# A cross-attention and mixture-of-experts layer: output tiles handled inside the last attention turns, and another way to list the experts' tokens

## The reference, cut to what matters

```python
# x (16, 112, 256); context (16, 375, 256); 16 heads of 16; 8 experts, 256 -> 512 -> 256
x = x + attention(layernorm(x), ctx, ctx, mask, Wq, bq, Wk, bk, Wv, bv, Wo, bo)
flat = layernorm(x).reshape(1792, 256)
probs = softmax(flat @ router_w)                      # (1792, 8)
topk_w, topk_idx = top_k(probs, 2);  topk_w /= clip(sum(topk_w), 1e-9)
y_e = silu(flat @ w1[e]) @ w2[e]                      # expert e
x = x + sum over the two chosen experts of weight * y_e
```

## Time and profile before

| | |
|---|---|
| median of 3 runs | 522.26 us (521.93 to 522.46) |
| the profiled execution | 520.47 us |
| its span, first to last instruction | 518.3 us |
| PE busy | 424.2 us, 82% |
| DVE, ACT, POOL busy | 348.9, 262.6, 189.3 us |
| mean granted TensorE clock | 0.896 of full |
| chain that ended last | PE 74%, DVE 9%, DMA 4%, ACT 4%, POOL 2% |

### The profile page before, as it was taken

One profiled execution on the slowest core, in us unless ns is written; L12 is line 12 of the kernel. 1 busy time (PEld: TensorE's weight loads), 2 busy tenths in 40 slices (PEclk: granted clock), 3 DMA queues, 4 the chain that ended last, 5 costly groups with the idle time before them and its releaser, 6 DMA issues.

```text
span 518.3 us, 10586 instructions
## 1 busy us (share of the span) xinstructions
PE 424.2 (82%) x4151; PEld 391.1 (75%) x4151; DVE 348.9 (67%) x743; ACT 262.6 (51%) x338; POOL 189.3 (37%) x162
## 2 busy tenths in 40 slices
PE   2666689999999999999996758445799999999800
PEld 2454489999999999999885657345799999999800
DVE  2776557788788788877871296474667667777427
ACT  3230245666666566666555204101877777777500
POOL 8270462222222222222100430007277777776410
PEclk9796779999999999999999687655999999999965
DMA  7949658676666677775604398002022222221158
GB/s 179 220 145 282 181 149 161 136 143 148 134 146 136 147 152 151 151 151 124 122 4 145 103 393 307 10 1 81 32 82 83 92 82 90 84 91 63 52 166 289
DMA packets 60609, 70.08 MB, mean 135 GB/s; under 512 B 19313, under 2 KB 55681, under 8 KB 60561
## 3 DMA queue, kind: packets, MB, share of 16 engines
q1 hardware_dynamic: 48224, 48.18, 39.8%
q0 software_dynamic: 4032, 11.02, 6.3%
q10 hardware_dynamic: 8304, 10.23, 5.6%
HBM read 35.64 MB, written 15.04 MB: 98 GB/s over the span
## 4 chain that ended last, share of the span: by engine, by line
PE 74%; DVE 9%; issue 5%; DMA 4%; ACT 4%; POOL 2%; SPq 1%; POOLq 0%; DVEq 0%; ACTq 0%
PE ps L1268 39%; PE ps L1329 11%; PE ps L1344 9%; PE ps L1358 8%; PE ps L1558 2%; ACT probs L678 2%; DMA y_back<-y_rows 2%; PE ps L1371 1%; SPq L477 1%; DVE x_rows_sb L927 1%; PE ps L1548 1%; DVE neg_max L880 1%; PE ps L1508 1%; DVE stats L916 1%; PE ps L1381 1%
## 5 line engine op out<-in xcount | busy, mean ns | idle before, releaser
L880 DVE TENSOR_REDUCE neg_max<-ps 112x1 f32<-112x376 f32 x256 | 133.7, 545 | 39.1 <-PE ps L1329 34.0
L678 ACT ACTIVATE probs<-ps 125x1344 f32<-125x1344 f32 x64 | 82.7, 1292 | 42.4 <-PE ps L1344 36.5
L1329 PE MATMUL ps<-k_stack,q_stack 98*112 98x376 f32 x256 | 89.2, 383 | 10.1 <-issue 6.0
L508 POOL TENSOR_TENSOR k_lo<-k_f,k_hi 128x752 fp32r<-128x752 f32 x16 | 28.8, 1802 | 139.2 <-ACT k_hi L652 136.7
L617 POOL DMA_INDIRECT y_rows<-y_out,slot_of_row x42 | 53.2, 1266 | 37.2 <-ACT y_out L814 30.8
L609 POOL DMA_INDIRECT rows<-xn_rows,token_of_row x42 | 42.9, 1021 | 61.2 <-DVE token_of_row L1142 47.5
L1329 PEld LDWEIGHTS ps<-k_stack,q_stack 98*112 98x112 f32 x256 | 45.7, 181 | 24.1 <-DVE neg_max L880 13.4
L1344 PE MATMUL ps<-q_stack,k_stack 100*125 100x224 f32 x384 | 53.6, 276 | 3.3 <-ACT probs L678 3.0
L1344 PEld LDWEIGHTS ps<-q_stack,k_stack 100*125 100x125 f32 x384 | 51.2, 191 | 5.1 <-ACT probs L678 4.9
L1268 PE MATMUL ps<-w_hi,h_hi 128*128 128x256 f32 x168 | 49.0, 292 | 3.1 <-issue 1.6
L1268 PE MATMUL ps<-flat_t_hi,w_hi 128*128 128x256 f32 x168 | 48.8, 290 | 2.8 <-DVE flat_t_lo L1179 2.8
(11 more groups left out here) (189 smaller groups left out, 974.1 us busy)
## 6 DMA issues: line engine op xcount, KB each, us to landing
k_stack<-k_hi SPq DMA_DIRECT2D x64, 188.0 KB, 4.5
w_all<-w ACTq DMA_DIRECT2D x16, 512.0 KB, 8.4
k_stack<-k_lo SPq DMA_DIRECT2D x32, 188.0 KB, 5.4
ctx_raw<-ctx_t SPq DMA_DIRECT2D x32, 187.5 KB, 5.1
q_stack<-q_scratch SPq DMA_DIRECT2D x32, 168.0 KB
q_scratch<-q_hi SPq DMA_DIRECT2D x16, 224.0 KB, 3.1
y_back<-y_rows SPq DMA_DIRECT2D x14, 256.0 KB, 5.5
q_scratch<-q_lo SPq DMA_DIRECT2D x8, 224.0 KB, 2.9
```

What stands on the lines that cost most here:

```text
L508: pool.tensor_tensor(kl[:, :, :], kf[:, :, :], kh[:, :, :].bitcast(F32), ALU.subtract)\
L678: act.activation(pf[j % 2][:, :, :], ps[0:CT, BK_ST:BK_ST + KT, 0:4 * S], ACT.Exp).then_inc(pf_ready, 1)
L880: dve.tensor_reduce(neg_max[:, s:s + 1], ps[0:S, BK_MAX + s % 2, 0:CP], AX.X, ALU.max, negate=True).then_inc(max_read, 1)
L1329: pe.matmul(ps[0:S, BK_MAX + a, 0:CP], qs[b.ring][0:R_MAX, q, S * a:S * (a + 1)], ks[b.ring][0:R_MAX, q, :], start=True, stop=True).then_i ...
```

## The change

**Tiles in groups.** The 14 tiles become 8 units (`UNITS`: six of two tiles, two of one). Unit 0 and 1 are projected by PE in turn 13, in the slots where the key projections stood, units 2 and 3 in turn 14. The last turns 15 and 16 are written out as one list in which units 4 to 7 are projected and all units are transposed and routed between the remaining scores and outputs. A unit's logits come straight out of `route` as 128 rows by 8 (the transposed tile is now the stationary operand), which removes the padded router weights, the ACT copy and `logits_back`. `x2` is loaded in turn 10 and its bias added by POOL after turn 12. The Newton steps are replaced by a power on POOL, which also normalises the first six units. The weight loads move from ACT's queue to two DMAs of 4 MB on SP's queue, issued between the writes of the normalised rows.

**Early and late tiles.** Expert choice, ranks and places are computed for tiles 0 to 11 first and then for tiles 12 and 13.

**Lanes.** A lane is a block of 128 places of an expert, 14 for each of 8 experts, 112 in all. POOL builds 28 tiles of 128 x 112 that hold a token's slot number at its lane, PE multiplies them with `is_place` in 28 products, and one more product maps the lanes to the 42 blocks. Slot numbers are 2 x token + choice, so the two outputs of a token lie side by side in `y_rows`, and the read-back is 7 DMAs with 2 KB pieces. `weigh` moves behind expert step 3.

The diff, cut to its core:

```diff
+UNITS = ((0, 2), (2, 2), (4, 2), (6, 2), (8, 2), (10, 2), (12, 1), (13, 1))
+GROUPS = ((0, 4), (4, 2), (6, 1), (7, 1))
+EARLY_NT = 12
+REACH = T // P
+ER = E * REACH
...
             for b in range(B):
+                if b == 10:
+                    sp.wait_ge(qproj_done, 2 * NG)
+                    sp.dma_start(x2[:, :, :], x_tiles.rearrange("n p d -> p n d")).then_inc(x2_in, 16)
                 turn(Batch(0, b))
-            sp.wait_ge(vproj_done, 2 * B)
-            sp.dma_start(x2[:, :, :], x_tiles.rearrange("n p d -> p n d")).then_inc(x2_in, 16)
...
+            for u in range(0, 4):
+                write_rows(u)
+            sp.wait_ge(st_done, QUADS * B)
+            sp.dma_start(w1_all[:, :, :].rearrange("p e (k n) -> p (e k) n", k=KD),
+                         w1.rearrange("e k p n -> p (e k) n")).then_inc(w1_in, 16)
+            for u in range(4, 6):
+                write_rows(u)
+            sp.wait_ge(ot_ready, B)
+            sp.dma_start(w2_all[:, :, :].rearrange("p e (k n) -> p (e k) n", k=KF),
+                         w2.rearrange("e k p n -> p (e k) n")).then_inc(w2_in, 16)
+            for u in range(6, 8):
+                write_rows(u)
...
-                for c in range(TOP):
-                    sp.dma_start(y_back[c][:, 2 * g:2 * g + 2, :],
-                                 y_rows[c * T + g * TG:c * T + (g + 1) * TG, :].rearrange("(n p) d -> p n d", p=P))\
-                        .then_inc(y_in[g], 16)
+                sp.dma_start(y_back[:, 2 * g:2 * g + 2, :, :],
+                             y_rows[TOP + TOP * TG * g:TOP + TOP * TG * (g + 1), :]
+                             .rearrange("(n p c) d -> p n c d", p=P, c=TOP)).then_inc(y_in[g], 16)
...
+            def roots(g):
+                first, n = GROUPS[g]
+                tiles = slice(tiles_of(first).start, tiles_of(first + n - 1).stop)
...
+                pool.tensor_tensor(row_rstd[:, tiles], row_var[:, tiles], minus_half[:, tiles], ALU.pow)\
+                    .then_inc(row_rstd_ready, 1)
+            def normalise_rows(u):
+                pool.wait_ge(row_rstd_ready, 1 if u < 4 else 2)
+                if u >= RINGS:
+                    pool.wait_ge(ft_done, u - RINGS + 1)
+                    pool.wait_ge(xn_written[u % RINGS], 16)
+                for a, n in enumerate(range(tiles_of(u).start, tiles_of(u).stop)):
+                    last = pool.tensor_scalar(xn2[u % RINGS][:, a, :], x2[:, n, :], mo2[:, n, 0:1], row_rstd[:, n:n + 1],
+                                              ALU.subtract, ALU.mult)
+                last.then_inc(early_xn_ready, 1)
+            def lanes(tiles, known):
+                pool.wait_ge(lanes_known, known)
+                for c in range(TOP):
+                    for n in range(tiles.start, tiles.stop):
+                        last = pool.tensor_scalar(placed[:, c, n, :], place_no[:, 0:ER], lane_of[:, c, n:n + 1],
+                                                  slot_no[:, c, n:n + 1], ALU.is_equal, ALU.mult)
+                last.then_inc(lanes_ready, 1)
+            for b in range(B + 1):
+                turn(Batch(0, b))
+                if b == B - 4:
+                    pool.wait_ge(x2_in, 16)
+                    pool.wait_ge(vo_bias_in, 16)
+                    constants()
+                    for g in range(NT // 2):
+                        add_bias(g)
...
                 def keys(t, *halves):
                     if has(b.after(3)):
                         project_keys(b.after(3), t, halves)
+                    elif halves[-1] == KD - 1:
+                        project_output(2 * (b.n - B + 3) + t)
...
+            def fill_lanes(tiles):
+                pe.wait_ge(lanes_ready, 1 if tiles.start == 0 else 2)
+                for c in range(TOP):
+                    pe.wait_ge(places_ready, (0 if tiles.start == 0 else TOP) + c + 1)
+                    for n in range(tiles.start, tiles.stop):
+                        last = pe.matmul(ps[0:ER, BK_PLACED, 0:P], placed[:, c, n, :], is_place[:, c, n, :],
+                                         start=c == 0 and n == 0, stop=c == TOP - 1 and n == NT - 1)
...
+            quad_outputs(last.after(-1), 2)
+            quad_outputs(last.after(-1), 3)
+            quad_scores(last, 0)
+            project_output(4)
+            out_transpose(last.after(-1))
+            quad_scores(last, 1)
+            quad_outputs(last, 0)
+            project_output(5)
+            attn_transpose(last.after(-1))
+            quad_scores(last, 2)
+            flat_transpose(0)
+            quad_outputs(last, 1)
+            flat_transpose(1)
+            quad_scores(last, 3)
+            route(0)
...
+            route(5)
+            project_output(7)
+            route(6)
+            rank_early()
+            flat_transpose(7)
+            route(7)
+            fill_lanes(slice(0, EARLY_NT))
+            rank_late()
+            fill_lanes(slice(EARLY_NT, NT))
             list_rows()
...
+            flat_low(6)
+            find_two(early_tiles, 6)
+            count_early()
+            normalise_late(7)
+            read_logits(6)
+            flat_low(7)
+            place_rows(early_tiles, BK_RANK, 1)
+            read_logits(7)
+            find_two(late_tiles, 8)
+            for c in range(TOP):
+                places_in_block(c, early_tiles)
+            place_rows(late_tiles, BK_LATE, 2)
+            for c in range(TOP):
+                places_in_block(c, late_tiles)
+            count_blocks()
+            blocks_of_lanes()
+            read_lanes()
+            list_tokens()
+            plan_steps()
             for n in range(-1, STEPS + 1):
                 expert_step(Batch(0, n))
+                if n == 3:
+                    weigh()
```

More of the change, by code:

```diff
@@ L146, in xattn_moe_kernel @@
         cursor["at"] = shared
+        x2 = sb("x2", [P, NT, D])
+        assert cursor["at"] <= q_end, "x2 lies where the transposed rows were"
+        cursor["at"] = q_end
+        attn_start = cursor["at"]
         expert_even = expert_buffers(0)
-        cursor["at"] = max(q_end, cursor["at"])
-        attn_start = cursor["at"]
+        late_start, cursor["at"] = cursor["at"], attn_start
+        placed = sb("placed", [P, TOP, NT, ER], F32R)
+        assert cursor["at"] <= attn_start + 6 * KD * CP * 4, "lanes lie where the context's parts were"
+        cursor["at"] = attn_start
         c_raw = [sb(f"ctx_raw{p}", [P, KD, CP]) for p in range(2)]
@@ L190, in xattn_moe_kernel @@
         keep = sb("keep", [P, B, CP], U8)
-        cursor["at"] = attn_start
-        x2 = sb("x2", [P, NT, D])
-        assert cursor["at"] <= attn_start + 6 * KD * CP * 4, "x2 lies where the context's parts were"
+        cursor["at"] = late_start
         w1_all = sb("w1_all", [P, E, KD * F])
@@ L230, in xattn_moe_kernel @@
-        listed = sb("listed", [P, NB])
-        spare = sb("spare", [P, NB])
-        token_i = sb("token_of_row", [P, NB], I32)
-        second_base = sb("second_base", [P, NB])
-        slot_base = sb("slot_base", [P, NB])
-        spare_slot = sb("spare_slot", [P, NB])
-        slot_i = sb("slot_of_row", [P, NB], I32)
-        nw = [sb(f"newton{n}", [P, NT]) for n in range(4)]
+        assert cursor["at"] <= xr_at, "the outputs lie where the probabilities were"
+        cursor["at"] = xr_at
@@ L238, in xattn_moe_kernel @@
+        is_place = sb("is_place", [P, TOP, NT, P], F32R)
+        assert cursor["at"] <= last_ring_end, "places lie where the last ring was"
+        cursor["at"] = last_ring_end
+        ones = sb("ones", [P, P], F32R)
+        earlier = sb("earlier", [P, P], F32R)
+        block_of_lane = sb("block_of_lane", [P, NB], F32R)
+        lane_tokens = sb("lane_tokens", [P, P], F32R)
+        slot_i = sb("slot_of_row", [P, NB], I32)
+        token_i = sb("token_of_row", [P, NB], I32)
         st2 = sb("stats2", [P, NT, 6])
@@ new lines, in _ @@
+            row_vars(0, row_stats(3))
+            normalise(last.after(-1))
+            residual(4)
+            row_stats(4)
+            attn_low(last.after(-1))
+            residual(5)
+            row_vars(1, row_stats(5))
+            flat_low(0)
+            read_logits(0)
+            flat_low(1)
+            read_logits(1)
+            flat_low(2)
+            read_logits(2)
+            residual(6)
+            row_vars(2, row_stats(6))
+            normalise(last)
+            flat_low(3)
@@ new lines, in _ @@
+            read_logits(3)
+            flat_low(4)
+            attn_low(last)
+            read_logits(4)
+            flat_low(5)
+            normalise_late(6)
+            read_logits(5)
+            residual(7)
+            row_vars(3, row_stats(7))
+            flat_low(6)
[6 more added lines that the diff above has]
+            read_logits(7)
```

665 lines of the change are left out of this document (354 added, 311 removed).

## The result

The changed kernel takes **538.06 us** (median of 4 runs, 534.11 to 538.65), the kernel before beside it 522.1 (520.04 to 522.46): a ratio of 1.030, with an interval of 1.025 to 1.035. I had forecast 518.1 with a range of 510.5 to 525: slower where I said faster, and 13 us outside the range. The profiled execution was the quickest of the changed kernel's runs, 534.11 us, with a span of 532.4 against 518.3.

What follows compares the result with a forecast made beforehand. A chain stepping from engine to engine, with no engine the bound: 6.7 us lost in the turns, 11.2 gained to the list, 0.9 lost by `weigh`, 0.6 gained in the tail, 4.2 faster; forecast 518.1 us, range 510.5 to 525.

Steps and rivals of the forecast that it cites:

- x2 in turn 10: Turn 10's load of x2 delays the stacked keys, so PE waits 2.0 us before turn 11; bounds 0 and 3.1.
- Turns 13 and 14: Two units of 12 products lengthen each of these turns by 2.0 us, together 3.9; bounds 2.0 and 5.8.
- Late `k_lo`: POOL's constants and bias additions delay batch 15's low part and turn 14's first head: cost 0.8 us, bounds 0 and 1.6.
- Last turn to unit 7's projection: From the last turn's outputs to unit 7's projection end: 30.9 us at full clock, 35.8 at half from unit 3, 33.4 taken.
- From there to the lanes: Unit 7's residual and variance, choice, early ranking and places, one after the other, from 33.4 to 44.2 us.
- Early lanes: POOL builds 24 lanes tiles at 0.33 us each, 7.9 us, ending at 52.1; bounds 0.22 and 0.42 each.
- The rival that named this: POOL's lanes are the bound: above 0.48 us each the kernel is slower than before, at 0.8 it takes 531; chance 0.13.
- Behind the lanes: From 52.1 to the list at 64.1 us: filling lanes, late ranking and places, four late lanes tiles, reading the lanes.
- `weigh`: Ten DVE instructions, 2.9 us, behind expert step 3, of which 0.9 us reaches PE; bounds 0 and 2.
- Tail: Seven read-back loads instead of 14 close DVE's first gap: 0.6 us gained, 1.9 if both gaps go, possibly 0.
- the gain to the list: From the last turn's start to the list, 64.1 instead of 75.3 us: 11.2 gained, bounds 5.4 and 16.8.

Runs made afterwards that it cites:

- the kernel with the last turn filled: The changed kernel plus 51 products of ones in PE's waits of the last turn, results unread; 529.09 us, ratio 1.018 to the kernel before.

## Why the prediction was wrong

Two steps of the prediction failed: the price of a lanes instruction on POOL, and the length of the last turn, whose clock fell sooner and cost more than I allowed. By its own steps, on the profiled execution:

- **x2 in turn 10**: 2.0 predicted, bounds 0 and 3.1; 3.04 measured. The mechanism was right, the bound too narrow: in the profiles of seven of the kernels built on this one PE's clock falls after that wait, and the turn loses up to 8.2. A wait was priced as its length alone. The first packet of the load came 1.25 us after its issue, not 1.9.
- **Turns 13 and 14**: 3.9 predicted, 3.5 measured (14.68 and 14.69 against 12.95 and 12.94).
- **Late `k_lo`**: 0.8 predicted, nothing seen. The low part came at 260.6 to 262.4, but PE was late itself by then; its head at 266.8 did not wait.
- **Last turn to unit 7's projection**: 33.4 predicted, top 35.8; 41.8 measured. This step failed. I let the clock fall from unit 3 on and gave that 4.9 us; it fell at the end of the first route. In the kernel with the last turn filled the same stretch, with the clock full, is 32.7, 1.8 us above my 30.9; the other 9 us went with the clock. POOL's normalised tiles at 1.2 us (predicted 0.4 to 0.8) and its power at 1.7 made one of them, 1.04 us.
- **From there to the lanes**: 10.8 predicted, 11.1 measured.
- **Early lanes**: 24 x 0.33 = 7.9 predicted, 20.45 measured. This step failed too, with the largest error, 12.5 us. 9.4 of it is the price: the instructions start 0.72 us apart. 3.1 is the one that stood beside `is_place`; I had put DVE's work beside POOL's at nothing. For the price I scaled rows of one input and constants by their element count alone. A part that doesn't scale is half of it: at idle 0.73 us for 112 elements and 1.21 for 256 leave about 0.36 at none. The rival that named this had its break-even at 0.48 and its time for 0.8 us at 531; 0.85 came on average. Its chance of 0.13 was too small, since "no POOL row shows two columns and two operations" was a reason to widen the bound, not to scale the nearest row.
- **Behind the lanes**: 12.0 predicted, 12.4 measured, with the late lanes at 3.2 instead of 1.3 and the rest shorter. The late ranking behind PE's wait was seen and not priced as something that could be moved: 5 us.
- **`weigh`**: 0.9 predicted, 1.8 measured, inside its bounds.
- **Tail**: 0.6 predicted, 1.6 won (24.1 to 22.5), of which the merged loads with their larger pieces are 1.3. The weight loads had moved at 390 and 385 GB/s in pieces of 2 KB and 1 KB; the read-back, at 384 and 342, doesn't bear out that the piece makes no difference.
- **Not in the sum**: the steps' rows at another address, 0.10 to 0.14 us a step.

Behind the list I had 0.3 lost and 3.0 were won. From the last turn's start to the list the sum is 8.4 + 0.3 + 12.5 + 0.4 = 21.6 late; less the 3.3, the forecast of 516.3 becomes 534.6 against 534.1 measured. The median is 4 above that profile; why stays open. (The lower bound of the gain to the list, 5.4, does not follow from its own terms: half clock and 0.42 us give 6.3.)

The Trainium skill's rate for POOL (GPSIMD Engine Reference, Performance versus the Vector engine) gave 0.2 to 0.3 us (0.17 to 0.24, if its 1.8 to 2.6 cycles are worked out at its 1.2 GHz, an estimate) and erred further than the rows did. By the two forms of a product of tensors, 0.34 and 0.58 us, POOL takes 1.7 ns an element, 2.0 cycles, which lies between its figures, though the page has the upper one for two inputs; the additions' 1.25 us for 512 elements are 2.9 cycles and not quite in agreement with it. With two operations POOL takes 3.3 ns, and that section gives no price for what comes before the first element, which here is 0.15 to 0.36 us. Its rule that elementwise work is DVE's was the one to follow: 0.25 against 0.73.

## What to carry over

An instruction with no row of its own form needs a bound from fixed cost and slope, not from scaling; where it stands N times in a row on the chain, N times the fixed cost decides. Look at shortest, median and longest of such a row before explaining its mean: here one of 24 took 3.1 us too many, beside a long instruction of another engine. A PE wait costs its length and can cost, behind it, what a fallen clock takes from the products, so several short waits between narrow products can be dearer than one long one (here 6.3 us in waits of at most 1.4 went with 9 us lost to the clock, a single wait of 5.5 with 2.7), and products into a part of PSUM that nobody reads are a cheap cure to try. In an in-order queue look for work that waits for nothing but its place: here it was worth 5 us.

## What the runs showed of the hardware

- 51 idle products in the last turn kept TensorE's granted clock at 1.00 where it was 0.50 for 24 of 27 us, and saved 9 us. No single wait of PE there had been longer than 1.4 us. In one of the three other kernels with these products it still fell, at 308.1 us for 10.2. The Trainium skill (TensorE: Matmul & The Clock Gate, A second HAM failure mode: psum-queue depth-cycling) tells of a kernel in which frequent short idles between groups of products made the clock swing between its two levels; the changed kernel's trace, at half, full and half again within 27 us, agrees.
- Products of 256 columns started 0.113 to 0.114 us apart, and 0.119 to 0.120 with their moving operand, by the kernels' own layout, some 41 KB lower in the partition. What of the address does it was not tried.
- POOL: 0.73 us for a two-operation instruction on 112 elements with two columns, 1.63 for a power of 8 columns and 0.52 for one, 0.17 for a product of 8 columns.
- One such POOL instruction took 3.87 us instead of 0.73 while DVE compared two tensors into 128 x 1536 elements twice (`is_place`, 3.42 us); a late one took 1.00 beside two of 128 x 256. Beside DVE's small instructions the lanes instructions of the changed kernel took 0.73 to 0.76.
